# Two transposes of YG taken behind the sixteen products of PV in a fused attention, state-space and expert kernel

## The reference

```python
# 1: attention of each image with itself (8 sequences of 1024 tokens)
q = inputs * dw1 @ pw1 + b1;  v = inputs * dw2 @ pw2 + b2
out = softmax(q @ q.T) @ v * gamma + inputs
# 2: t = out + block(layernorm(out)); the block is a state-space layer
z, xBC, dt = split(rmsnorm(x) @ W_in.T)
xBC = silu(causal_conv4(xBC) + conv_b)          # xs (8 heads of 32), B, C
state = state * exp(dt * A) + dt * x_t B_t      # per head, token after token
y = state @ C_t + Dp * xs
y = rmsnorm(y * silu(z)) * gnorm_w
block = x + y @ W_out.T
# 3: t = t + experts(layernorm(t)): 8 experts, the best 2 of each token
```

## Time and profile before

| | |
|---|---|
| median of 3 runs | 1213.07 us (1212.02 to 1215.37) |
| the profiled execution | 1216.53 us, its span 1214.8 us |
| TensorE busy | 1060.8 us, 87% of the span |
| VectorE, ScalarE, GpSimd busy | 838.7, 744.9, 611.1 us |
| granted clock of TensorE, mean | 0.945 of full |

### The profile page before, as it was taken

How to read it: one execution, slowest core, us unless ns; L and a number is a source line. 1 busy time by engine, 2 the same in 40 slices (tenths; PEclk the granted TensorE clock), 3 DMA queues, 4 the chain that set the end, 5 groups by cost and what they waited for, 6 DMA issues and landing times.

```text
span 1214.8 us, 29800 instructions
## 1 busy us (share of the span) xinstructions
PE 1060.8 (87%) x8280; PEld 978.3 (81%) x8281; DVE 838.7 (69%) x2991; ACT 744.9 (61%) x1869; POOL 611.1 (50%) x972
## 2 busy tenths in 40 slices
PE   3899999999999999999999999872199999999940
PEld 2679888888888888988988988761199999999940
DVE  3488889888988988988888888754344444444434
ACT  1567677677777777767767767532066666666520
POOL 7123443567467557557556567546444444444420
PEclk8999999999999999999999999885599999999975
DMA  7100000001001001000100000000222222222259
GB/s 224 32 1 27 11 1 28 8 21 41 11 23 38 13 23 35 12 27 10 36 21 15 21 11 15 14 9 29 60 60 63 61 65 61 63 64 61 61 139 302
DMA packets 73319, 55.21 MB, mean 45 GB/s; under 512 B 9941, under 2 KB 67837, under 8 KB 73213
## 3 DMA queue, kind: packets, MB, share of 16 engines
q1 hardware_dynamic: 55581, 32.15, 9.9%
q0 software_dynamic: 8448, 17.45, 4.4%
q10 hardware_dynamic: 9184, 4.33, 1.2%
HBM read 31.21 MB, written 23.22 MB: 45 GB/s over the span
## 4 chain that ended last, share of the span: by engine, by line
PE 60%; issue 12%; POOL 10%; DVE 9%; ACT 3%; DMA 3%; SPq 1%; ACTq 0%; POOLq 0%; DVEq 0%
PE pc L363 7%; PE pX L512 7%; PE pY L517 7%; PE pa L413 5%; PE pb L525 3%; PE pd L525 3%; PE pY L329 3%; PE pc L367 2%; DVE CV L1059 2%; PE pX L342 2%; PE pa L374 2%; POOL rows_by_expert L899 2%; PE pX L344 2%; PE pX L343 2%; PE pb L435 1%
## 5 line engine op out<-in xcount | busy, mean ns | idle before, releaser
L911 POOL DMA_INDIRECT results_by_choice<-YE,DIX x136 | 130.2, 957 | 169.3 <-ACT YE L706 161.4
L1324 DVE TENSOR_TENSOR V<-XT,pY 128x384 f32<-128x384 f32 x136 | 75.4, 554 | 141.1 <-ACT XT L697 119.1
L899 POOL DMA_INDIRECT rows_by_expert<-XA,SL x128 | 147.4, 1151 | 41.2 <-issue 36.8
L363 PEld LDWEIGHTS pc<-XDT,M 128*128 128x128 f32 x1024 | 125.3, 194 | 12.3 <-issue 8.0
L1059 DVE SCALAR_TENSOR_TENSOR CV<-XBC,cw,CV 128x256 f32<-128x256 f32 x288 | 132.0, 512 | 0.0
L363 PE MATMUL pc<-XDT,M 128*128 128x64 f32 x1024 | 123.9, 275 | 5.0 <-DVE CT L1065 5.0
L413 PE MATMUL pa<-V,PT 128*128 128x128 f32 x1024 | 127.6, 278 | 0.0
L413 PEld LDWEIGHTS pa<-V,PT 128*128 128x128 f32 x1024 | 119.8, 192 | 2.3 <-issue 0.3
L839 POOL TENSOR_TENSOR YG<-Y,SZ 128x256 f32<-128x256 f32 x64 | 46.6, 728 | 139.7 <-DVE Y L1093 125.6
L1070 DVE TENSOR_REDUCE NM<-pX 128x1 f32<-128x1024 f32 x64 | 78.0, 1219 | 54.8 <-PE pX L344 53.2
L512 PE MATMUL pX<-TA,XBC 128*128 128x128 f32 (+1 forms) x816 | 114.3, 276 | 1.3 <-ACT XBC L693 0.7
(11 more groups left out here) (265 smaller groups left out, 2874.9 us busy)
## 6 DMA issues: line engine op xcount, KB each, us to landing
GX<-rows_by_expert SPq DMA_DIRECT2D x136, 65.0 KB
XT<-in_xT_dram SPq DMA_DIRECT2D x8, 512.0 KB, 4.0
X<-in_x_dram SPq DMA_DIRECT2D x16, 256.0 KB, 3.0
W<-results_by_choice SPq DMA_DIRECT2D x8, 512.0 KB, 8.7
out_dram<-T ACTq DMA_DIRECT2D x8, 512.0 KB, 6.8
results_by_choice<-YE,DIX POOLq DMA_INDIRECT x136
rows_by_expert<-XA,SL POOLq DMA_INDIRECT x128
W<-in_w1T_dram SPq DMA_DIRECT2D x1, 1364.0 KB
```

What stands on the lines that cost most here:

```text
L363: mm(pc[:, 64 * h:64 * h + 64], M[:, h, :], XDT[:, e % 2, HD * h:HD * h + 64], start=h == 0, stop=False, skip_group_check=True)
L899: g.indirect_dma_start(xg, bass.IndirectOffsetOnAxis(ap=SL[:, j // NT, j % NT:j % NT + 1], axis=0), XA[:, j // NT, j % NT, :], None).then_ ...
L911: g.indirect_dma_start(yg, bass.IndirectOffsetOnAxis(ap=DIX[:, j, :], axis=0), YE[:, j, :], None).then_inc(s(f"ye{j}_scattered"), 16)
L1324: tt(HT[:, par].rearrange("p k t -> p (k t)"), SH[:, par, :], pY[:, 512 * par:512 * par + HP3], ALU.mult).then_inc(s("hh_ready"), 1)
```

## The change

The block under `if there(base, e):` with the two transposes of YG and the three waits ahead of it stands behind the block with PV, no longer ahead of it. Two blocks that only the first batch has (a wait in step 3, three small products in step 5) keep their place ahead of PV. Nothing else is changed.

```diff
                     last.then_inc(s("d_ps"), 1)
+                if base == 0 and i == 3:
+                    pe.wait_ge(s("setup"), 1)
...
+                if there(base, o):
+
+                    upto(pe, "pt_act", base, o + 1)
+                    upto(pe, "xdt_ready", base, k + 1)
+                    upto(pe, "gT_ready", base, k + 1)
+                    upto(pe, "t_ready", base, o)
+                    for j in range(NT):
+                        last = mm(pa[:, 0:C], PT[:, P * j:P * j + P], V[:, j, :], start=j == 0, stop=j == NT - 1)
+                    last.then_inc(s("o_ps"), 1)
                 if there(base, e):
                     upto(pe, "yg_ready", base, e + 1)
                     upto(pe, "t2_ready", base, e)
...
                     for m in range(2):
                         last = nc.tensor.transpose(pb[:, P * m:P * m + P], YG[:, P * m:P * m + P], ident[:])
                     last.then_inc(s("yT_ps"), 1)
-                if base == 0 and i == 3:
-                    pe.wait_ge(s("setup"), 1)
...
-                if there(base, o):
-
-                    upto(pe, "pt_act", base, o + 1)
-                    upto(pe, "xdt_ready", base, k + 1)
-                    upto(pe, "gT_ready", base, k + 1)
-                    upto(pe, "t_ready", base, o)
-                    for j in range(NT):
-                        last = mm(pa[:, 0:C], PT[:, P * j:P * j + P], V[:, j, :], start=j == 0, stop=j == NT - 1)
-                    last.then_inc(s("o_ps"), 1)
                 if front_a:
```

More of the change, by code:

```diff
@@ L390, in step @@
                     last.then_inc(s("d_ps"), 1)
[L391 to L398, removed]
                 if base == 0 and i == 3:
@@ L414, in step @@
                     last.then_inc(s("o_ps"), 1)
+                if there(base, e):
+                    upto(pe, "yg_ready", base, e + 1)
+                    upto(pe, "t2_ready", base, e)
+                    if front_b:
+                        upto(pe, "u_ready", base, fb + 1)
+                    for m in range(2):
+                        last = nc.tensor.transpose(pb[:, P * m:P * m + P], YG[:, P * m:P * m + P], ident[:])
+                    last.then_inc(s("yT_ps"), 1)
                 if front_a:
```

## The result

The changed kernel takes 1242.47 us (median of 4 runs, 1240.48 to 1243.88), the kernel before, measured beside it, 1214.22 us. The ratio is 1.023 with a 95% interval of 1.0202 to 1.0258: 28 us slower. The profiled execution took 1240.48 us, its span is 1238.7 us and its mean granted clock 0.95.

A forecast was written before the change was run, and what follows sets the result against it. TensorE, at nine tenths or more busy at full clock, was taken to bound the tile loop. Gross 41.9 us less 11.7 back gives net 30.2; on 1213.07 that makes 1243 us, range 1230 to 1256.

The forecast's parts named there:

- (a): Ahead of PV: PV waits for XDT, starting 0.10 us behind it; odd steps 0.10 sooner, batch starts 0.31, even unchanged.
- (b): Behind PV: uncovered chain transposes, YT, output product; even steps 0.91 us later, odd and batch starts 0.60; gross 41.9 us.
- (c): Work queued behind: YT moves about 1.3 us on ScalarE in even steps; ED's chain is untouched, VectorE's LR not held.
- (d): TensorE's existing waits for VectorE, mainly before L353 and L342, take up part of the delay: 11.7 us back.
- (e): New TensorE gaps of about 0.6 us (even steps) and 0.4 (odd) leave the clock full, 2.4 GHz.
- The rival on the other side: Faster: if VectorE set every step's period, only PV's earlier start would count, 4.8 us, giving 1208 us; 4 in 100.

## Why the prediction was right

The forecast was 1243, the measurement 1242.47. That they agree to half a microsecond is in part luck: the forecast was a rise of 30 on a kernel before of 1213.07, the measurement a rise of 28.3 on 1214.22. For the loop alone the forecast 30.2 stands against 30.0 up to step 63. Its steps can be held against the rows one by one.

- *(a) PV stands at XDT.* Right: 0.10 to 0.11 in every step from 7 to 64, the value that I took.
- *(b) The chain behind PV.* Right in kind, and two sizes were off in opposite directions. From transposes to product I had 0.91; it is 0.85 to 0.86, because YT follows the YG transposes after 0.42, not after 0.47 as XNT follows those of XN. And the exposed weight load of the product, 0.11, was missing. Together an even step pays 0.85 + 0.11 = 0.96 for my 0.91 (in step 2, where L427 waits, 0.95); an odd one 3.54 - 2.78 - 0.10 = 0.66 for my 0.60.
- *(c) What is queued.* Right: LR and PT aren't held. But the margin that I gave for LR, over a microsecond, was read from an odd step alone. In steps 4 and 6 of the changed kernel LR starts 0.88 and 0.95 behind the start of the product, and in the kernel with the second copy, where LR is 0.16 and 0.09 later behind PV, 0.77: the room there was only 0.11 and 0.18.
- *(d) What comes back.* In kind right, a little larger in size. In regular batches (medians over steps 16 to 56; L353 counted from L350's start less 0.46, L342 from L329's start less 0.82, what each takes without a wait) the wait before L353 goes from 0.57 to 0.06 behind step 3 and from 0.78 to 0.10 behind step 7 (I had 0.2 left), that before L342 from 0.69 to 0.34 behind step 6 and from 0.18 to 0.01 behind step 4. A batch, from PV in step 32 to PV in step 40, takes 99.58 for 95.47: 4.1 longer, forecast 3.9. Two errors cancel in part: gross it is 6.2 for my 5.7, and 2.1 come back for my 1.8.
- *(e) The clock.* Right: full through the loop; in the step from 63 to 64, where the kernel before has 0.88, the changed one has 1.00. A window of the changed kernel (us, busy PE, PEld, DVE, ACT, POOL, granted clock, DMA share, GB/s):

```profile
400.00:500.00 100.00, 95.43 (x715) 84.97 (x714) 82.85 (x298) 71.04 (x167) 57.75 (x101) 1.00 0.08 23
```

  The same window of the kernel with the second copy, whose gaps are 0.28 us longer:

```profile
400.00:500.00 100.00, 93.45 (x703) 83.46 (x700) 81.41 (x292) 71.72 (x171) 56.67 (x99) 1.00 0.08 23
```

  The clock stays at 2.4 GHz through both.

  The rule in the Trainium skill, "TensorE: Matmul & The Clock Gate", section "A second HAM failure mode: psum-queue depth-cycling", that short idles between groups of products can make the clock go back and forth, is not borne out at the gaps that these kernels have, 0.3 to 0.8 us once a step. The page's case has bf16 products with 512 columns, and no run here is of that kind.
- *The rival on the other side* was given too much: even with the transposes taken out and PV free to start early, the loop gains 1.6 us, where I had reckoned 4.8 for it. I hadn't seen that in odd steps YT, behind ED on ScalarE, is the next thing that holds TensorE.

What stays open: of a batch's 6.2 us of gross delay (3 x 0.96, 4 x 0.66 and the first step's 0.7) 2.1 come back. The four waits above explain 1.7, and in the step behind step 2 waits before L363 (0.15) and L367 (0.08) another 0.2; the last 0.2 I haven't traced. In the profiled spans the difference is only 23.9 us against 30.0 in the loop; the changed kernel gained 1.4 of the rest in the step from 63 to 64, with the fuller clock, and what remains lies behind or ahead of the loop, where the profiles scatter by more than that. The medians of the runs differ by 28.3.

## What to carry to other kernels

A short producer, copy, consumer chain through another engine is free only as long as TensorE has independent work between its ends; the length to cover is the whole round trip plus the consumer's first weight load, here about 1 us, and what is missing is paid in each turn of the loop in which no later wait takes it up. Look for both covers that a piece gives: these transposes were covered by PV behind them and themselves covered the wait for XDT ahead, so that at their old place they cost nearly nothing. What fills a gap must not itself wait for the result, as the counting products do, and must keep the result early enough for its next reader, which is what made the kernel with the product at the end of the step slower than the changed one.

## What the runs showed of the hardware that I had not expected

- The output product that starts on a released wait for YT, its stationary operand, holds TensorE 0.11 us longer: the four instructions of L435 take 0.57 to L307 in place of 0.46. Their first weight load starts with the product (533.34 both) and not 0.11 ahead of it (528.63 and 528.74).
- ScalarE, idle both times, starts its copy 0.42 us after the start of the YG transposes (into pb) and 0.47 to 0.48 after that of the XN transposes (into pc), which have the same shapes. What makes the difference I did not try.
- Two copies of 128x256 from PSUM on ScalarE, each 0.38 long in its row, start 0.28 apart (403.46 and 403.74).
